# A ramp table written on chip, two small loads on ScalarE's queue, and an earlier place for the first values

## The chip, the cores and the metric

The kernel runs on one core of one Trainium2 chip. The metric is the device time of one execution in microseconds. TensorE is called PE in the rows, VectorE DVE, ScalarE ACT, GpSimd POOL and SyncE SP.

## The reference

One transformer-like block on x of shape (8, 128, 256), all float32:

```
k  = layernorm(x);  v = ctx_2048
y  = wkv(w, u, k, v)          # a scan over the 128 steps, per channel
x1 = x + tanh(g_xattn) * y
f  = fwht(layernorm(x1) * SU_ug) / 64
h  = silu(f @ W_gate.T * (Wscale_gate * 64)) * (f @ W_up.T * (Wscale_up * 64))
out = x1 + tanh(g_ffn) * (fwht(h * SU_dp) / 64 @ W_down.T * (Wscale_dp * 64))
```

In wkv the state decays by exp(w) per step, where w is negative; the numerator collects exp(k)·v and the denominator exp(k), and y is their quotient. For w above zero the kernel adds a correction to k that grows linearly with the step number: minus max(w, 0) times the ramp 0, 1, 2, ... 127.

## The kernel before

The batch of 8 sequences is cut into four groups (0 to 3) of two sequences, 256 tokens each. Every group goes through the same stages: layer norm of x on token rows (`stats1`, `rstd1`, `norm1`), a transposition by PE that puts channels on partitions (`keys`), exp (`keys` on ScalarE), a scan of the denominator (`scan_a`, `mix_den`), the product with the values (`av`), a scan of the numerator (`scan_av`, `mix_num`), a reciprocal by Ln and Exp with one Newton step (`recip`, `error`, `estimate`, `newton`), x1 (`x1`), the Hadamard product (`fwht`), its norm (`square`, `ones`, `rstd2`, `root`, `f_scaled`, `f_hi`, `f_lo`), and then eight slots of gate, up and down products on PE (L900, L938). Each float32 product of the slots is made of three fp32r products of high and low parts.

The weights are prepared on chip in the same head: gate and up weights are transposed and split (`w`, `w_rest`, `w_hi`, `w_lo`), and the down weights go through a Hadamard transformation of butterflies (`fly`, on GpSimd) and PE products (`m`, `m_rest`). So the first 33 us hold the work of group 0 and the preparation, and from there the slots follow one another.

The order on each engine is written out by hand in four tables (`PE_STAGES`, `ACT_STAGES`, `DVE_STAGES`, `POOL_STAGES`); an engine does its list in order and waits on semaphores. On VectorE the head is: stats1 0, setup_rows, norm1 0, setup_shift, stats1 1, center 0, scan_a 0, mix_den 0, av 0, scan_av 0, mix_num 0, norm1 1, estimate 0, newton 0, x1 0, and then the groups after it. On PE it is: keys 0, center, w 0, w_rest 0, w 1, w 2, w 3, w_rest 1 to 3, keys 1, fwht 0, m 0, ones 0, keys 2, m 1. On GpSimd, after eleven memsets: rstd1 0, rstd1 1, fly 0 to 2, error 0, fly 3 to 6.

All loads are issued by SyncE, in this order: the x of group 0 (X, 256 KB), VT (vectors, 17 KB), VR (the row of w, 1 KB), HI (Hadamard and identity matrices, 128 KB), STEP (the ramps, 68 KB, from the host), the x of group 1, the first half of the gate weights (WN, 512 KB), the down weights (DN, 1024 KB), the first half of the up weights (512 KB), the values of group 0 (V, 258 KB), the transposed x of group 0 (XT, 256 KB), the two other halves of the weights, and then the rest of x, V and XT.

The linear correction is a product in `keys` on PE (L809): WPLUS (the negated max(w, 0), its rounded part on partitions 0 and 1, its remainder on partitions 32 and 33) with STEPR, the ramps. `setup_rows` on VectorE makes WPLUS (L612, L615, L619), and the stage `setup` on ScalarE copies STEP to STEPR (L476) after two table loads and two tanh.

Of the kernel before, what the change touches and what calls it, by code (L numbers as in the profile page):

```python
# [5 lines left out]
F32 = mybir.dt.float32  # L6
F32R = mybir.dt.float32r
ALU = mybir.AluOpType
ACT = mybir.ActivationFunctionType

P = 128
NB = 8
C = 256
INTER = 1024
CT = C // P
JT = INTER // P
GB = 2
NG = NB // GB
GT = GB * P
# [116 lines left out]
ON_ACT = {n: places(ACT_STAGES, n) for n in SHARED}  # L136


def build(nc, x, xt, ct, vecs, rows, consts, steps, weights, w_down, out):
    with ExitStack() as stack:  # L140
        def sb(name, shape, dt=F32):
            return stack.enter_context(nc.sbuf_tensor(name, shape, dt))
# [4 lines left out]
        def sem(name):  # L147
            return stack.enter_context(nc.semaphore(name))
# [2 lines left out]
        XT = sb("XT", [P, NG, CT, GT])  # L151
        V = sb("V", [P, NG, CT, GB, PAD])
        VT = sb("VT", [P, NV])
        VR = sb("VR", [CT, P])
        HI = sb("HI", [P, 2 * P])
        HN = sb("HN", [P, P])
        STEP = sb("STEP", [32 + CT, CT, GT])
        STEPR = sb("STEPR", [P, CT, GT], F32R)
        NEGW = sb("NEGW", [CT, P])
        WPLUS = sb("WPLUS", [P, P], F32R)  # L160
        TG = sb("TG", [P, 2])
        DEC, SUMU, CUR, RATIO, MPOS, NEGM, OUTS = (sb(n, [P, CT]) for n in ("DEC", "SUMU", "CUR", "RATIO", "MPOS", "NEGM", "OUTS"))
        NHALF = sb("NHALF", [P, GB])
# [39 lines left out]
        KZ = bank("KZ")  # L203
# [4 lines left out]
        x_in = [sem(f"x{i}_in") for i in range(3)]  # L208
        xt_in = [sem(f"xt{i}_in") for i in range(3)]
        ctx_in = [sem(f"ctx{i}_in") for i in range(3)]  # L210
        const_in, vec_in, row_in, step_in, down_in, stored = (sem(n) for n in ("const_in", "vec_in", "row_in", "step_in", "down_in", "stored"))
        w_in = {(m, h): sem(f"w{m}{h}_in") for m in range(2) for h in range(2)}

        step_clear, plus_clear, pads, d_clear, half, eps_set, ones_set = (sem(n) for n in (
            "step_clear", "plus_clear", "pads", "d_clear", "half", "eps_set", "ones_set"))
        tanh_gate, decay_low, c_ready, m_ready, ratio_ready, decay_set, padded_set, alpha, outs = (sem(n) for n in (
            "tanh_gate", "decay_low", "c_ready", "m_ready", "ratio_ready", "decay_set", "padded_set", "alpha", "outs"))
        neg_ready, signs, wplus, steps_r, centers, at_ready = (sem(n) for n in (
            "neg_ready", "signs", "wplus", "steps_r", "centers", "at_ready"))
# [153 lines left out]
        @block.sync  # L373
        def _(sp):
            def load_x(i):
                b = slice(GB * i, GB * (i + 1) if i < 2 else NB)
                sp.dma_start(X[:, b, :], x[:, b, :]).then_inc(x_in[i], 16)

            def load_xt(i):
                g = slice(i, i + 1 if i < 2 else NG)  # L380
                sp.dma_start(XT[:, g, :, :], xt[:, g, :, :]).then_inc(xt_in[i], 16)

            def load_ctx(i):
                g = slice(i, i + 1 if i < 2 else NG)
                sp.dma_start(V[:, g, :, :, :], ct[:, g, :, :, :]).then_inc(ctx_in[i], 16)

            def load_w(m, h):
                j = slice(h * JT // 2, (h + 1) * JT // 2)
                sp.dma_start(WN[:, m, j, :], weights[:, m, j, :]).then_inc(w_in[m, h], 16)  # L389

            load_x(0)
            sp.dma_start(VT[:, :], vecs).then_inc(vec_in, 16)
            sp.dma_start(VR[:, :], rows).then_inc(row_in, 16)
            sp.dma_start(HI[:, :], consts).then_inc(const_in, 16)
            sp.dma_start(STEP[:, :, :].rearrange("p t n -> p (t n)"), steps).then_inc(step_in, 16)
            load_x(1)
            load_w(0, 0)
            sp.dma_start(DN[:, :, :], w_down).then_inc(down_in, 16)
            load_w(1, 0)
            load_ctx(0)  # L400
            load_xt(0)
            load_w(0, 1)
            load_w(1, 1)
            load_x(2)
            load_ctx(1)
            load_xt(1)
            load_ctx(2)
            load_xt(2)
            for g in range(LAST):
                sp.wait_ge(out_ready, CT * (g + 1))  # L410
                sp.dma_start(out[:, g, :, :], XT[:, g, :, :]).then_inc(stored, 16)
            for t in range(CT):
                sp.wait_ge(out_ready, CT * LAST + t + 1)
                sp.dma_start(out[:, GROUPS[LAST][0]:NG, t, :], XT[:, GROUPS[LAST][0]:NG, t, :]).then_inc(stored, 16)
            sp.wait_ge(stored, 16 * (LAST + CT))

        @block.gpsimd
        def _(pool):
            pool.memset(NHALF[:, :], -0.5).then_inc(half, 1)
            pool.memset(D[:, :, :, :], 0.0).then_inc(d_clear, 1)  # L420
            pool.memset(D0[:, :, :, :], 0.0).then_inc(d_clear, 1)
            pool.memset(STEPR[:, :, :].bitcast(F32), 0.0).then_inc(step_clear, 1)
            pool.memset(WPLUS[:, :].bitcast(F32), 0.0).then_inc(plus_clear, 1)
            pool.memset(SQ[:, 0:1], 0.0).then_inc(pads, 1)
            pool.memset(SP_[:, 0:1], 0.0).then_inc(pads, 1)
            pool.memset(EA[:, :, :, :, 0:1], 0.0).then_inc(pads, 1)
            pool.memset(MEAN[:, :].bitcast(F32), 1.0 / C).then_inc(ones_set, 1)
            pool.memset(ONES[:, :], 1.0 / C).then_inc(ones_set, 1)
            pool.memset(EPSC[:, :], EPS * C).then_inc(eps_set, 1)

            def stage(name, g):
                if name == "rstd1":

                    pool.wait_ge(half, 1)
                    pool.wait_ge(ve1, g + 1)
                    pool.tensor_tensor(RS1[:, GB * g:GB * (g + 1)], VE1[:, GB * g:GB * (g + 1)], NHALF[:, :], ALU.pow).then_inc(rstd1, 1)
                elif name == "fly":
                    fly(pool, g, by_pool["fly"])
                elif name == "norm1":
                    normalise(pool, g, by_pool["norm1"])  # L440
                elif name == "w_lo":
                    split_weight(pool, g, by_pool["w_lo"])
                elif name == "av":
                    multiply_values(pool, g, by_pool["av"])
                elif name == "error":
                    reciprocal_error(pool, g, by_pool["error"])
                elif name == "x_lo":
                    split_x1(pool, g, by_pool["x_lo"])
                elif name == "sum":

                    pool.wait_ge(squared, CT + g)
                    if g > 1:
                        pool.wait_ge(v_full, g)
                    pool.tensor_tensor(FSUM[:, :], FSQ[:, 0, :], FSQ[:, 1, :], ALU.add).then_inc(summed, 1)

            for q in range(-1, SLOTS):
                if q >= 0:

                    n = width(q)
                    pool.wait_ge(h_hi, q + 1)  # L460
                    pool.tensor_tensor(HL[:, q % JT, 0:n], ring(H, q), HH[:, q % JT, 0:n].bitcast(F32), ALU.subtract).then_inc(h_lo, 1)  # L461
                for name, g in POOL_STAGES.get(q, []):
                    stage(name, g)

        @block.scalar
        def _(act):
            def stage(name, g):
                if name == "setup":
                    act.preload_act_table_set("exp_and_others")
# [1 line left out]
                    act.activation(TG[:, 0:1], VT[:, V_GATE:V_GATE + 1], ACT.Tanh, scale=-1.0).then_inc(tanh_gate, 1)  # L471
                    act.activation(TG[:, 1:2], VT[:, V_GATE + 1:V_GATE + 2], ACT.Tanh).then_inc(tanh_gate, 1)
                    act.preload_act_table_set("natural_log_exp_and_others")
                    act.wait_ge(step_clear, 1)
                    act.wait_ge(step_in, 16)
                    act.activation(STEPR[0:32 + CT, :, :], STEP[:, :, :], ACT.Copy).then_inc(steps_r, 1)  # L476

                elif name == "decay":

# [128 lines left out]
        def _(dve):  # L608
            def setup_rows():

                dve.wait_ge(row_in, 16)
                dve.tensor_scalar(NEGW[:, :], VR[:, :], 0.0, -1.0, ALU.max, ALU.mult).then_inc(wplus, 1)  # L612
                dve.wait_ge(wplus, 1)
                dve.wait_ge(plus_clear, 1)
                dve.tensor_copy(WPLUS[0:CT, :], NEGW[:, :]).then_inc(wplus, 1)  # L615
                dve.wait_ge(vec_in, 16)
                dve.tensor_scalar(DEC[:, :], VT[:, V_W:V_W + CT], 0.0, None, ALU.min).then_inc(decay_low, 1)
                dve.wait_ge(wplus, 2)
                dve.tensor_tensor(WPLUS[32:32 + CT, :], NEGW[:, :], WPLUS[0:CT, :].bitcast(F32), ALU.subtract).then_inc(wplus, 1)  # L619

            def setup_shift():

# [168 lines left out]
        def _(pe):  # L791
            def stage(name, g):
                if name == "keys":
# [12 lines left out]
                        pe.wait_ge(wplus, 3)  # L806
                        pe.wait_ge(steps_r, 1)
                    for t in range(CT):
                        i = pe.matmul(KZ[:, t * GT:(t + 1) * GT], WPLUS[:, :], STEPR[:, t, :], start=False, stop=True, skip_group_check=True)  # L809
                    i.then_inc(k_turned, 1)  # L810
                elif name == "center":

# [5 lines left out]
                elif name == "m":  # L818
# [5 lines left out]
                    for i in range(2):  # L824
                        had = HN[:, :] if i and g // 2 else HAD
                        n = 4 * i + 2 * (g % 2)
# [190 lines left out]
```

## Time and profile before

| what | value |
|---|---|
| three timed executions | 117.4, 118.2, 118.34 us; median 118.2 |
| profiled execution, first to last instruction (span) | 117.3 us |
| profiled execution's own time outside the span | the page gives none; the lowest of the three times is 0.1 us above the span, the median 0.9 us |
| busy PE / DVE / ACT / POOL | 99.5 / 70.0 / 67.6 / 61.3 us |
| granted TensorE clock, mean | 0.999 |
| DMA | 7.69 MB, mean 66 GB/s |

The span is what the views of the trace cut into pieces. Busy shares are means over the whole span: in the first quarter PE is about half busy and the DMA engines are full from 5 to 21 us; from 36 us on PE is busy nearly without a break.

### The profile page before, as it was taken

The page shows a single profiled execution, that of the slowest core. Times are in us where ns is not written, and L with a number is a line of the kernel's source. Part 1 is how long each engine was busy: PE and PEld are TensorE (multiplying, and loading weights), DVE is VectorE, ACT ScalarE, POOL GpSimd, SP SyncE. Part 2 cuts the span into 40 slices and gives each one's busy share as a digit, 9 for nine tenths or more (in the row PEclk, how much of TensorE's full clock was granted, in tenths as well). Part 3 has the DMA queues.
Part 4 walks back from the last instruction along what each step waited for, and adds up shares of the span by engine and source line. Part 5 has one row for each costly group of instructions (what it writes and reads, how often), then busy time and mean ns, then how long its engine had stood idle before and what let it go on. Part 6 is the DMA issues. An engine that isn't in the chain of part 4 may idle for free.

```text
span 117.3 us, 1942 instructions
## 1 busy us (share of the span) xinstructions
PE 99.5 (85%) x684; PEld 89.2 (76%) x684; DVE 70.0 (60%) x145; ACT 67.6 (58%) x146; POOL 61.3 (52%) x76
## 2 busy tenths in 40 slices
PE   0056584799969999999999999999999999869980
PEld 0044463664559978789999999999999999769970
DVE  0688289936696798797998456874137531231311
ACT  4589566013689942999562899645459732504400
POOL 7102899689909897953550805732520633222430
PEclk9999999999999999999999999999999999999999
DMA  2799999200000000000000020000020000020002
GB/s 72 171 329 409 334 399 408 101 0 3 0 3 6 0 0 0 0 0 6 0 0 0 3 95 0 0 0 0 6 89 0 3 0 6 0 89 0 3 0 89
DMA packets 3074, 7.69 MB, mean 66 GB/s; under 512 B 468, under 2 KB 854, under 8 KB 2936
## 3 DMA queue, kind: packets, MB, share of 16 engines
q1 hardware_dynamic: 3064, 7.57, 17.9%
q8 instruction: 5, 0.08, 0.3%
q14 instruction: 5, 0.04, 0.1%
HBM read 6.52 MB, written 1.05 MB: 65 GB/s over the span
## 4 chain that ended last, share of the span: by engine, by line
PE 70%; DMA 9%; DVE 8%; ACT 4%; SPq 3%; issue 2%; POOL 1%; POOLq 1%; ACTq 0%; DVEq 0%
PE UG L900 38%; PE OD L938 12%; DMA V<-in_ct 9%; PE KZ L938 6%; PE UG L827 5%; PE FX L859 5%; PE FX L868 2%; DVE X L327 1%; DVE XT L762 1%; PE VB L876 1%; DVE SP_ L640 1%; SPq L389 1%; ACT S L596 1%; DVE OD L705 1%; PE VB L881 1%
## 5 line engine op out<-in xcount | busy, mean ns | idle before, releaser
L461 POOL TENSOR_TENSOR HL<-H,HH 128x256 fp32r<-128x256 f32 x32 | 25.7, 813 | 32.4 <-ACT HH L587 32.4
L776 DVE SCALAR_TENSOR_TENSOR H<-S,ALPHA,UG 128x256 f32<-128x256 f32 x32 | 15.0, 478 | 22.3 <-ACT S L596 22.1
L596 ACT ACTIVATE S<-UG,VT 128x256 f32<-128x256 f32 x32 | 15.1, 472 | 17.5 <-PE UG L900 17.4
L900 PE MATMUL UG<-FH,WTH 128*128 128x256 f32 x128 | 21.4, 289 | 0.8 <-ACT FH L581 0.8
L900 PE MATMUL UG<-FL,WTH 128*128 128x256 f32 x128 | 20.4, 281 | 0.0
L900 PE MATMUL UG<-FH,WTL 128*128 128x256 f32 x128 | 20.3, 280 | 0.0
L900 PEld LDWEIGHTS UG<-FH,WTH 128*128 128x128 f32 x128 | 17.8, 189 | 2.1 <-issue 1.9
L900 PEld LDWEIGHTS UG<-FH,WTL 128*128 128x128 f32 x128 | 17.4, 189 | 0.0
L900 PEld LDWEIGHTS UG<-FL,WTH 128*128 128x128 f32 x128 | 17.4, 188 | 0.0
L587 ACT ACTIVATE HH<-H 128x256 fp32r<-128x256 f32 x32 | 13.2, 412 | 4.5 <-DVE H L776 4.2
L938 PE MATMUL OD<-HH,MH 128*128 128x256 f32 x40 | 11.3, 283 | 1.6 <-DVE XT L762 1.6
L938 PE MATMUL OD<-HH,ML 128*128 128x256 f32 x40 | 11.2, 281 | 0.0
L938 PE MATMUL OD<-HL,MH 128*128 128x256 f32 x40 | 11.2, 280 | 0.0
L803 PE MATMUL KZ<-HI,X 128*128 128x128 f32 x16 | 3.4, 353 | 8.4 <-DVE X L327 8.2
L803 PEld LDWEIGHTS KZ<-HI,X 128*128 128x128 f32 x16 | 2.4, 179 | 9.2 <-issue 8.7
L938 PEld LDWEIGHTS OD<-HH,MH 128*128 128x128 f32 x40 | 7.6, 189 | 1.8 <-DVE XT L762 1.8
L938 PEld LDWEIGHTS OD<-HL,MH 128*128 128x128 f32 x40 | 7.5, 189 | 0.0
L938 PEld LDWEIGHTS OD<-HH,ML 128*128 128x128 f32 x40 | 7.5, 188 | 0.0
L938 PE MATMUL KZ<-HH,MH 128*128 128x256 f32 x24 | 6.9, 289 | 0.4 <-POOL HL L461 0.3
L342 POOL TENSOR_TENSOR DEN<-DEN,R 128x512 f32<-128x512 f32 x4 | 5.2, 1291 | 3.9 <-ACT R L521 3.9
L827 PE MATMUL UG<-DN,HI 128*128 128x512 f32 x12 | 7.1, 712 | 0.0
L938 PE MATMUL KZ<-HH,ML 128*128 128x256 f32 x24 | 6.7, 280 | 0.0
(120 smaller groups left out, 200.5 us busy)
## 6 DMA issues: line engine op xcount, KB each, us to landing
WN<-in_weights SPq DMA_DIRECT2D x4, 512.0 KB, 9.8
DN<-in_w_down SPq DMA_DIRECT2D x1, 1024.0 KB, 8.6
out<-XT SPq DMA_DIRECT2D x3, 256.0 KB, 2.5
V<-in_ct SPq DMA_DIRECT2D x2, 258.0 KB, 10.8
V<-in_ct SPq DMA_DIRECT2D x1, 516.0 KB, 12.5
X<-in_x SPq DMA_DIRECT2D x2, 256.0 KB, 4.2
XT<-in_xt SPq DMA_DIRECT2D x2, 256.0 KB, 10.8
X<-in_x SPq DMA_DIRECT2D x1, 512.0 KB, 11.5
```

Source lines behind the costliest of these rows:

```text
L327: i = eng.tensor_scalar(X[:, n, :], X[:, n, :], MV1[:, n, 0:1], RS1[:, n:n + 1], ALU.subtract, ALU.mult)
L342: eng.tensor_tensor(lanes(DEN[:, g % 2, :, :, :]), lanes(DEN[:, g % 2, :, :, :]), lanes(R0[:, g % 2, :, :, :]), ALU.mult).then_inc(done, 1)
L461: pool.tensor_tensor(HL[:, q % JT, 0:n], ring(H, q), HH[:, q % JT, 0:n].bitcast(F32), ALU.subtract).then_inc(h_lo, 1)
L587: act.activation(HH[:, q % JT, 0:n], ring(H, q), ACT.Copy).then_inc(h_hi, 1)
L596: act.activation(ring(S, q), gate_part(q), ACT.Silu, scale=VT[:, V_SGATE + j:V_SGATE + j + 1]).then_inc(silu_ready, 1)
L776: dve.scalar_tensor_tensor(out=ring(H, q), in0=ring(S, q), scalar=ALPHA[:, j:j + 1], in1=up_part(q), op0=ALU.mult, op1=ALU.mult).then_inc( ...
L803: pe.matmul(KZ[:, t * GT + b * P:t * GT + (b + 1) * P], X[:, GB * g + b, t * P:(t + 1) * P], IDENT, is_transpose=True, start=(t == 0 and b ...
L827: a = pe.matmul(fill(item)[:, :], had, DN[:, n:n + 2, :].rearrange("p j c -> p (j c)"), start=(i == 0), stop=False, skip_group_check=True)
L859: i = pe.matmul(FX[:, o * GT:(o + 1) * GT], AT[:, o, t, :].bitcast(F32), XT[:, g, t, :], start=(o == t == 0), stop=(t == CT - 1), skip_gro ...
L868: i = pe.matmul(FX[:, o * GT:(o + 1) * GT], AT[:, o, t, :], part[:, t, :], start=(n == o == t == 0), stop=(n == 1 and t == CT - 1), skip_g ...
L900: return pe.matmul(dst.rearrange("p (g n) -> p g n", n=GT), w[:, m, j, t, :], f[:, chunks, t, :], start=start, stop=stop, skip_group_check ...
L938: a = pe.matmul(total(g, t), m[:, j, t * P:(t + 1) * P], h[:, j, 0:n], start=(j == 0 and k == 0 and (t == 0 or g == LAST)), stop=(j == JT ...
```

## The change

The ramps are no longer loaded. One ramp of 256 elements (0 to 127, twice) is written to all 128 partitions of STEP by an iota on GpSimd, in place of the memset of STEPR; ScalarE copies it to STEPR, 128x256 in place of 34x512. WPLUS becomes 256 wide with w in one row (partition 0 the rounded part, partition 32 the remainder), and each of the two products of L809 takes its half of WPLUS and the same ramp. VT and VR are issued by ScalarE ahead of its first table load. SyncE issues X group 0, HI, V group 0, the first gate half, X group 1, XT group 0, DN, the first up half, and the rest as before.

```
-            sp.dma_start(VT[:, :], vecs).then_inc(vec_in, 16)
-            sp.dma_start(VR[:, :], rows).then_inc(row_in, 16)
             sp.dma_start(HI[:, :], consts).then_inc(const_in, 16)
-            sp.dma_start(STEP[:, :, :].rearrange("p t n -> p (t n)"), steps).then_inc(step_in, 16)
+            load_ctx(0)
+            load_w(0, 0)
             load_x(1)
-            load_w(0, 0)
+            load_xt(0)
             sp.dma_start(DN[:, :, :], w_down).then_inc(down_in, 16)
             load_w(1, 0)
-            load_ctx(0)
-            load_xt(0)
...
-            pool.memset(STEPR[:, :, :].bitcast(F32), 0.0).then_inc(step_clear, 1)
+            pool.iota(STEP[:, :].rearrange("p (b q) -> p b q", b=GB), [[0, GB], [1, P]], 0, 0, allow_small_or_imprecise_dtypes=True).then_inc(steps_set, 1)
...
         @block.scalar
         def _(act):
+            act.dma_start(VT[:, :], vecs).then_inc(vec_in, 16)
+            act.dma_start(VR[:, :], rows).then_inc(row_in, 16)
...
-                    act.wait_ge(step_clear, 1)
-                    act.wait_ge(step_in, 16)
-                    act.activation(STEPR[0:32 + CT, :, :], STEP[:, :, :], ACT.Copy).then_inc(steps_r, 1)
+                    act.wait_ge(steps_set, 1)
+                    act.activation(STEPR[:, :], STEP[:, :], ACT.Copy).then_inc(steps_r, 1)
...
-                dve.tensor_copy(WPLUS[0:CT, :], NEGW[:, :]).then_inc(wplus, 1)
+                dve.tensor_copy(WPLUS[0:1, :], NEGW[:, :]).then_inc(wplus, 1)
...
-                dve.tensor_tensor(WPLUS[32:32 + CT, :], NEGW[:, :], WPLUS[0:CT, :].bitcast(F32), ALU.subtract).then_inc(wplus, 1)
+                dve.tensor_tensor(WPLUS[32:33, :], NEGW[:, :], WPLUS[0:1, :].bitcast(F32), ALU.subtract).then_inc(wplus, 1)
...
-                        i = pe.matmul(KZ[:, t * GT:(t + 1) * GT], WPLUS[:, :], STEPR[:, t, :], start=False, stop=True, skip_group_check=True)
+                        i = pe.matmul(KZ[:, t * GT:(t + 1) * GT], WPLUS[:, t * P:(t + 1) * P], STEPR[:, :], start=False, stop=True, skip_group_check=True)
```

## Rows read from the trace of the kernel before

**Rows 1.** The page, the chain that ended last, by engine and by line
```profile
PE 70%; DMA 9%; DVE 8%; ACT 4%; SPq 3%; issue 2%; POOL 1%; POOLq 1%; ACTq 0%; DVEq 0%
```
**Rows 2.** The chain in order of time: start us, us, what
```profile
4.76 10.09 DMA V<-in_ct
...
22.16 3.75 PE FX L859 x8
25.91 2.98 PE UG L827 x4
...
44.35 1.73 PE FX L859 x8
```
**Rows 3.** Timeline of VectorE, 11 to 22.2 us: start us, us, instruction [idle before]
```profile
11.76 0.88 DVE L698 SCALAR_TENSOR_TENSOR DEN<-OD,RATIO,SQ 128x256 f32<-128x256 f32 x2
14.87 0.70 DVE L337 TENSOR_TENSOR OD<-OD,V 128x512 f32<-128x512 f32 x1 [2.24 <-DMA V<-in_ct]
...
17.79 2.02 DVE L327 TENSOR_SCALAR X<-X,MV,RS 128x256 f32<-128x256 f32 x2
...
20.53 0.70 DVE L719 SCALAR_TENSOR_TENSOR OD<-DEN,OD 128x512 f32<-128x512 f32 x1
```
**Rows 4.** Timeline of all engines, 0 to 14 us, the same columns
```profile
1.16 0.42 SPq L392 DMA_DIRECT2D VT<-in_vecs  x1
...
1.63 0.32 SPq L393 DMA_DIRECT2D VR<-in_rows  x1
1.68 0.52 POOL L422 MEMSET STEPR<- 128x512 f32 x1
...
2.38 0.28 SPq L395 DMA_DIRECT2D STEP<-in_steps  x1
...
4.09 0.20 ACT L471 ACTIVATE TG<-VT 128x1 f32<-128x1 f32 x1 [2.10 <-DMA VT<-in_vecs]
...
5.07 0.21 DVE L612 TENSOR_SCALAR NEGW<-VR 2x128 f32<-2x128 f32 x1
...
5.32 0.79 POOL L436 TENSOR_TENSOR RS<-VE,NHALF 128x2 f32<-128x2 f32 x1 [2.53 <-DVE VE L674]
...
6.14 0.73 DVE L327 TENSOR_SCALAR X<-X,MV,RS 128x256 f32<-128x256 f32 x2 [0.23 <-POOL RS L436]
6.38 0.63 ACT L476 ACTIVATE STEPR<-STEP 34x512 fp32r<-34x512 f32 x1 [0.69 <-DMA STEP<-in_steps]
...
9.47 0.75 DVE L662 TENSOR_TENSOR AT<-GG,FX 128x256 fp32r<-128x256 f32 x2 [0.28 <-PE FX L816]
```
**Rows 5.** Timeline of PE, 6 to 34 us, the same columns
```profile
7.76 0.77 PE L809 MATMUL KZ<-STEPR,WPLUS 128*128 128x256 f32 x2
8.64 0.80 PE L816 MATMUL FX<-GG,MEAN 128*128 128x256 f32 x2
...
13.55 2.80 PE L841 MATMUL UG<-HI,WN 128*128 128x128 f32 x12 [1.24 <-DMA WN<-in_weights]
...
17.95 0.80 PE L848 MATMUL UG<-WTH,NI 128*128 128x512 f32 x1 [0.75 <-ACT WTH L536]
19.96 1.09 PE L803 MATMUL KZ<-HI,X 128*128 128x128 f32 x4 [1.21 <-DVE X L327]
20.70 0.78 PE L809 MATMUL KZ<-STEPR,WPLUS 128*128 128x256 f32 x2
```
**Rows 6.** Timeline of GpSimd, 11 to 36 us, the same columns
```profile
12.20 3.73 POOL L369 TENSOR_TENSOR DB<-DN 128x512 f32<-128x512 f32 x3 [2.17 <-DMA DN<-in_w_down]
15.88 1.28 POOL L342 TENSOR_TENSOR DEN<-DEN,R 128x512 f32<-128x512 f32 x1
```
**Rows 7.** Windows of the whole core: stretch, length, busy times, clock, DMA share, GB/s
```profile
4.00:5.00 1.00, 0.00 (x0) 0.00 (x0) 0.93 (x5) 0.89 (x3) 0.00 (x0) 1.00 0.62 82
5.00:10.00 5.00, 2.58 (x10) 2.04 (x11) 4.10 (x20) 4.31 (x13) 1.46 (x2) 1.00 0.97 331
```
**Rows 8.** The loads of the tile X, issue to landing
```profile
DMA to landing us min/median/max: 3.2/5.2/11.5
```

More of the change, by code:

```diff
@@ L136, with build @@
 ON_ACT = {n: places(ACT_STAGES, n) for n in SHARED}
-def build(nc, x, xt, ct, vecs, rows, consts, steps, weights, w_down, out):
+def build(nc, x, xt, ct, vecs, rows, consts, weights, w_down, out):
     with ExitStack() as stack:
@@ L153, in build @@
         VT = sb("VT", [P, NV])
-        VR = sb("VR", [CT, P])
+        VR = sb("VR", [1, C])
         HI = sb("HI", [P, 2 * P])
         HN = sb("HN", [P, P])
[L157 to L160, printed above, removed]
+        STEP = sb("STEP", [P, GT])
+        STEPR = sb("STEPR", [P, GT], F32R)
+        NEGW = sb("NEGW", [1, C])
+        WPLUS = sb("WPLUS", [P, C], F32R)
         TG = sb("TG", [P, 2])
@@ L210, in build @@
         ctx_in = [sem(f"ctx{i}_in") for i in range(3)]
-        const_in, vec_in, row_in, step_in, down_in, stored = (sem(n) for n in ("const_in", "vec_in", "row_in", "step_in", "down_in", "stored"))
+        const_in, vec_in, row_in, down_in, stored = (sem(n) for n in ("const_in", "vec_in", "row_in", "down_in", "stored"))
         w_in = {(m, h): sem(f"w{m}{h}_in") for m in range(2) for h in range(2)}
-        step_clear, plus_clear, pads, d_clear, half, eps_set, ones_set = (sem(n) for n in (
-            "step_clear", "plus_clear", "pads", "d_clear", "half", "eps_set", "ones_set"))
+        steps_set, plus_clear, pads, d_clear, half, eps_set, ones_set = (sem(n) for n in (
+            "steps_set", "plus_clear", "pads", "d_clear", "half", "eps_set", "ones_set"))
         tanh_gate, decay_low, c_ready, m_ready, ratio_ready, decay_set, padded_set, alpha, outs = (sem(n) for n in (
@@ L994 @@
     gates = np.concatenate([np.asarray(inputs["g_xattn"]), np.asarray(inputs["g_ffn"])])
-    steps = np.kron(np.eye(CT, dtype=np.float32), np.tile(np.arange(P, dtype=np.float32), GB))
     weights = np.stack([np.asarray(inputs["L0_ffn_W_gate"]), np.asarray(inputs["L0_ffn_W_up"])])
@@ L1002 @@
         "vecs": np.ascontiguousarray(np.concatenate([columns, np.broadcast_to(gates, (P, 2))], axis=1)),
-        "rows": np.ascontiguousarray(np.asarray(inputs["L0_xattn_w"]).reshape(CT, P)),
+        "rows": np.ascontiguousarray(np.asarray(inputs["L0_xattn_w"]).reshape(1, C)),
         "consts": np.ascontiguousarray(np.concatenate([hadamard(P), np.eye(P, dtype=np.float32)], axis=1)),
-        "steps": np.concatenate([steps, np.zeros((32 - CT, CT * GT), np.float32), steps]),
         "weights": np.ascontiguousarray(np.concatenate([
```

## The prediction

> **What bounds the kernel now.** I read the chain that ended last first. By engine it is 70% PE and 9% DMA [rows 1]; the DMA part is one piece in the chain's order of time, the load of V for group 0, 4.76 to 14.85 us [rows 2]. Behind it the chain runs over VectorE to x1, then into fwht 0 on PE at 22.16 us, the m 0 product at 25.91, and from 33 us over the slots, where PE has hardly a gap. So a microsecond won at 22.16 should stay to the end, as no load and no other engine is waited for in a way that doesn't shift with it.
>
> Next the timeline of VectorE. mix_den ends at 12.64, then VectorE stands for 2.24 us until V is there, and av 0 starts at 14.87 [rows 3]. Those 2.24 us are all that an earlier V can give there, since av comes after mix_den in VectorE's list. The rest of the prediction asks what else is late once V is early: the front up to scan_a, the norm1 1 and the Newton step on the way to x1, and PE's own list ahead of fwht 0.
>
> **V and the chain of group 0.** V moves from eighth or ninth place to third. In front of it stand X (256 KB) and HI (128 KB). It would be issued at about 1.6 us and even with the 5.2 us to landing of the middle X load [rows 8] it is there at 6.8 us, 5.8 us ahead of 12.64. So the wait of 2.24 us goes: **−2.24**. What follows takes from av 0 (14.87) to the end of x1 (22.01) 7.14 us, and one piece of it isn't fixed: the two instructions of norm1 1 took 2.02 us here against 0.73 for the same pair at 6.14 [rows 3, 4]. GpSimd was in its butterflies meanwhile. Bounds: 1.29 us better, or as much as one GpSimd instruction (1.28 [rows 6]) worse; I take 0, as GpSimd will be in the butterflies again, and it is the nearest row.
>
> **The front, to scan_a at 10.28.** The small edits:
> - VT and VR leave SyncE's queue and STEP goes: 0.47 + 0.36 + 0.33 = 1.16 us from one issue to the next are gone ahead of the large loads [rows 4]. On ScalarE they put 0.42 + 0.32 = 0.74 us ahead of its first table load; ScalarE idled 2.10 us behind that load, waiting for VT [rows 4], so this is hidden with 1.3 us to spare. VT itself is issued 0.44 us earlier. VT and X now run beside each other: 17 KB against 256 KB is 7% of X's 3.2 us [rows 8], so X group 0 lands between 0 and 0.2 us later; I take 0.1.
> - iota for the memset of STEPR: no row shows an iota. GpSimd starts the memset of 128x512 at 1.68 (0.52 us), ends its memsets at 2.79 and then idles 2.53 us [rows 4]. Nearest rows: a memset of half that size below, a two-operand instruction of 128x512 (1.28 us [rows 6]) above. Either way it is 0, cover 2.5 us. Beyond that each microsecond delays rstd1 0, and so everything. The wider memset of WPLUS adds 0.2 us at most in the same gap.
> - STEPR: ScalarE waited 0.69 us for STEP and copied for 0.63 us [rows 4]. The wait goes and the copy has half the columns (−0.2 to −0.3). So ScalarE's queue (signs, decay, pads) is about 0.9 us, with the earlier VT up to 1.3 us, ahead.
> - setup_rows on VectorE: three instructions on 1x256 in place of 2x128. The first took 0.21 us for 128 columns [rows 4], one of X's norm 0.37 for 256: +0.15 each, +0.45 in all, between 0 and 0.6. VectorE idled 0.23 us before norm1 0 for rstd1 0 [rows 4]; so +0.2 reach norm1 0.
> - The two L809 products keep their size, 0.77 us in keys 0 [rows 5]. Edits of names and the DRAM row of w cost nothing.
>
> What of this reaches scan_a? Before it on VectorE stands center 0, which waited 0.28 us for PE's centre product [rows 4, 5]. PE does keys 0 first. With X and norm1 0 later by 0.1 + 0.2, keys 0 ends at 8.8 instead of 8.53, centre starts at once (the signs are long there, 0.9 us ahead), where before it had waited for them: 8.8 against 8.64, +0.15. So ScalarE's gain of 0.9 us is worth nothing here, since PE and VectorE come last: **+0.1** with rounding.
>
> The third candidate is X group 1, which stats1 1 (7.95) takes ahead of center 0 in VectorE's list. It goes behind V and the first gate half, 770 KB more. At 331 GB/s, the rate from 5 to 10 us [rows 7], this is 2.3 us. Against it: the 1.16 us of issue, and a hole: from 4 to 5 us only 82 GB/s were moved, while STEP and the start of X group 1 were in the queue [rows 7], against 331 behind it, so about 0.7 us are lost. Sum: 7.9 + 2.3 − 1.16 − 0.7 = 8.3 us. The slack is 0.28 us (plus 0.15), up to about 8.3 us. **Cost 0**, bounds −0 and +0.7 (hole not regained).
>
> The Trainium skill, page "DMA: Bandwidth & Descriptors", section "Why a DMA increments its semaphore by 16 and not by 1", says that a load uses the largest number up to 16 of DMA engines that divides its outermost size. For the 34 rows of STEP that is two engines, which fits the hole in the row, and if these two were late in every load behind it, the gain from its removal would be larger than my sum counts. The same page, section "Issuing engines are not separate DMA queues", says that issuing from a second engine saves only the issue time; the 1.16 us of the row are then what the two queues and the dropped load can give.
>
> **The Newton step.** newton 0 (20.53) needs error 0 from GpSimd, which comes after three butterflies, and they wait for DN: 12.20 + 3.73, then 1.28, end 17.16 [rows 6], 5.0 us behind DN. DN goes behind V and XT: 514 KB more, 68 KB less, 446 KB at 331 GB/s: +1.35, less 1.16 and 0.7: it lands at 11.7 in place of 12.2 (11.5 to 13.4 with and without the two credits). error 0 then ends at 16.7, and newton would start at 20.53 − 2.1 = 18.4. It costs nothing until DN lands later than 13.4. XT goes forward too, and nobody waited for it before [rows 3].
>
> **PE's list ahead of fwht 0.** Once x1 is early, this is next. w 1 started at 13.55 after a wait of 1.24 us for the first up half; w_rest 3 ended at 18.75, then 1.21 us of wait for norm1 1, then keys 1 until 21.48, and 0.68 us for x1 [rows 5]. Without the waits keys 1 takes 1.52 us: fwht 0 can't start before the landing of the up half (13.45) + 5.3 + 0.1 + 1.52, that is landing + 6.9. The up half comes right behind DN in both orders, so −0.5 too: 12.95, floor 19.9. x1 ends at 22.01 − 2.24 + 0.1 = 19.9 + a little. So both arrive together. Bounds of the floor: landing 12.8 to 14.6, fwht 0 at 19.7 to 21.5; I take the same value as x1 gives, 20.05 with the usual 0.15 between x1 and PE.
>
> **Sum.** 22.16 − 20.05 = 2.1 us at fwht 0. Behind it m 0 needs butterflies 4 and 6 (they shift with DN, and it has 3.7 us behind fwht's start), keys 2 needs norm1 2, one or two microseconds early before. I cost these at 0; if GpSimd's list shifts by 1.4 instead of 2.1 the slack still covers it. Span 117.3 − 2.1 = 115.2; median 118.2 − 2.1 = **116.1 us**, as the median lies 0.9 above the profiled span.
>
> **Rivals.**
> 1. **TensorE's clock rises sooner.** The eight fwht records took 3.75 us at 22.16 and 1.73 us at 44.35, four m records 2.98 us at 25.91 [rows 2]. The granted column says 1.00 in both, but by the durations the first stretch ran at 1.2 GHz and the later at 2.4 GHz; the change of speed fell into m 0, near 28.5 us, after PE had been busy nearly without a break from 22.16. If with shorter waits between keys 1 and fwht 0 it comes a further 2 us of work sooner than my shift, 1 us more is won: 115.0. The Trainium skill, "TensorE: Matmul & The Clock Gate", section "What's actually happening", says that the clock rises once the array has been kept busy and that the look at it runs freely, not from the kernel's start. By that rule the place differs between executions, in either direction.
> 2. **The clock rises at the same 28.5 us.** Then the 2.1 us of work that would have come after it run at half speed: 1.05 of the gain are given back: 117.1.
> 3. **The loads give it back.** X group 1 lands at 9.0 (+0.7 on scan_a) or the up half at 14.6 (floor 21.5, gain 0.7), or a second GpSimd instruction blocks norm1 1 (+1.3): 117.1 to 117.8. For it: the DMA engines are full from 5 us on, so what is put forward pushes others back. Against: 1.8 us of credits.
> 4. **The change doesn't move V's wait**, another load holds av 0: 118.2. Hardly, since V stands third.
> 5. **The iota is slow**, the case on the slower side. GpSimd does it at 1.68 us ahead of rstd1 0. It decides from 2.5 + 0.5 = 3.0 us on; from there each microsecond goes through norm1 0, keys, scan_a. At 3.0 + 2.1 = 5.1 us the gain is gone; at 7 us the time is 120.1. The rows of GpSimd's instructions of 128x512 (0.52 and 1.28) speak against it; that no iota is in the trace is all that speaks for it.
>
> **Chances.** Forecast (115.3 to 116.9) 0.55; rival 1, 0.17; rival 2, 0.10; rival 3, 0.10; rival 4, 0.03; rival 5, 0.05. About 1% is what a measurement of this kernel tells from no change (117.0 to 119.4). Faster: 0.55 + 0.17 and a little of 3, 0.74; same 0.21; slower 0.05. The range for 8 in 10 takes rival 1 to its end and most of 2 and 3: 115.0 to 117.5.
>
> **What would show it.** In the new profile: the idle time before av 0 is gone and av 0 starts at 12.6 to 12.9; scan_a at 10.3 to 10.5; iota under 1.3 us and rstd1 0 still waiting for VectorE; stats1 1 at about 8.3; the butterflies start at 11.7 to 12.2; w 1 at 13; fwht 0 at 20.05; m 0's change of speed two to three us before 28.5; first slot near 31. The prediction is wrong if av 0 starts early and fwht 0 doesn't follow (PE's list or GpSimd), if scan_a moves by over half a microsecond, or if the stretch from fwht 0 to the end changes in length, which would be the clock.

## The result, and the profile after

The changed kernel takes 117.13 us (median of 20 runs, 115.72 to 117.98) and the kernel before 118.37 us (20 runs, 117.25 to 119.86): ratio 0.985, 95% interval 0.982 to 0.989, or about −1.7 us by the ratio and −1.2 by the medians. The two differ because the ratio leaves out executions more than 1.5% above the fastest of their kernel. The profiled execution took 116.77 us with a span of 115.0, so 1.8 us lie outside the span. The span before was 117.3. The gain is clear of noise, and small: 1.5%, with an interval that ends below 2%.

The page's chain that ended last, after, by engine, and then pieces of it in order of time (start us, us, what), against [rows 1, 2]:

```profile
PE 71%; DVE 15%; ACT 4%; DMA 4%; issue 2%; POOL 1%; POOLq 1%; DVEq 0%; ACTq 0%
```

```profile
0.72 4.10 DMA X<-in_x
...
20.41 3.75 PE FX L858 x8
24.17 2.37 PE UG L826 x4
```

V is out of the chain. The one load that weighs in it is the x of group 0, and VectorE has nearly twice the share. fwht 0 starts 1.75 us sooner than in [rows 2] and takes the same 3.75 us; the m 0 records behind it take 2.37 us instead of 2.98.

The timeline after, 0 to 38 us, for the lines of [rows 3 to 6]:

```profile
0.72 0.41 ACTq L464 DMA_DIRECT2D VT<-in_vecs  x1
...
1.62 0.42 SPq L385 DMA_DIRECT2D V<-in_ct  x1
...
1.78 0.35 POOL L419 IOTA STEP<- 128x256 f32 x1
...
4.85 0.75 DVE L667 BATCH_NORM_STATS2 BS<-X 128x6 f32<-128x256 f32 x2 [4.85 <-DMA X<-in_x]
5.02 0.20 ACT L471 ACTIVATE TG<-VT 128x1 f32<-128x1 f32 x1 [2.02 <-DMA VT<-in_vecs]
...
6.24 0.72 POOL L433 TENSOR_TENSOR RS<-VE,NHALF 128x2 f32<-128x2 f32 x1 [3.43 <-DVE VE L673]
...
6.63 0.42 ACT L475 ACTIVATE STEPR<-STEP 128x256 fp32r<-128x256 f32 x1
6.70 0.41 DVE L618 TENSOR_TENSOR WPLUS<-NEGW,WPLUS 1x256 fp32r<-1x256 f32 x1
...
7.14 0.74 DVE L327 TENSOR_SCALAR X<-X,MV,RS 128x256 f32<-128x256 f32 x2
...
8.75 0.75 DVE L667 BATCH_NORM_STATS2 BS<-X 128x6 f32<-128x256 f32 x2
...
10.67 1.22 DVE L639 TENSOR_TENSOR_SCAN SQ<-D,OD 128x512 f32<-128x512 f32 x1
...
11.66 3.74 POOL L369 TENSOR_TENSOR DB<-DN 128x512 f32<-128x512 f32 x3 [0.83 <-DMA DN<-in_w_down]
...
13.00 2.80 PE L840 MATMUL UG<-HI,WN 128*128 128x128 f32 x12 [0.46 <-DMA WN<-in_weights]
...
13.12 0.70 DVE L337 TENSOR_TENSOR OD<-OD,V 128x512 f32<-128x512 f32 x1
...
16.03 2.03 DVE L327 TENSOR_SCALAR X<-X,MV,RS 128x256 f32<-128x256 f32 x2
...
30.80 0.74 PE L899 MATMUL UG<-FH,WTH 128*128 128x256 f32 x4 [0.78 <-ACT FH L580]
```

The reader is to see two things. av 0 (L337) no longer waits. But stats1 0, the first row of VectorE, starts at 4.85: in the kernel before it starts at 3.93, and norm1 0 follows 2.2 to 2.3 us later in both (6.14 in [rows 4], 7.14 here). The delay is 1.0 us at norm1 0 and at keys 0, 0.80 at stats1 1, 0.70 at PE's centre product, 0.53 at center 0 and 0.39 at scan_a. That, and 0.1 us between mix_den and av 0, is why av 0 gained 1.75 us and not 2.24.

The windows after (columns as in [rows 7]) show the loads as an unbroken stream, 271 GB/s from 4 to 5 us where before there were 82:

```profile
4.00:5.00 1.00, 0.00 (x0) 0.00 (x0) 0.15 (x1) 0.00 (x0) 0.00 (x0) 1.00 0.98 271
5.00:10.00 5.00, 1.97 (x10) 2.00 (x11) 4.62 (x22) 4.87 (x15) 0.72 (x1) 1.00 1.01 369
```

### The profile page after: what moved, and what is told of

The parts are those of the page before. It is cut to its first block, busy times and chain, and to the rows that moved or that the text cites. A ratio compares the mean times of both kernels' runs of the same rounds, so it can differ in the third digit from the quotient of the medians.

```text
span 115.0 us, 1940 instructions
## 1 busy us (share of the span) xinstructions
PE 98.3 (85%) x684; PEld 88.9 (77%) x684; DVE 70.3 (61%) x145; ACT 67.5 (59%) x146; POOL 61.4 (53%) x76
## 3 DMA queue, kind: packets, MB, share of 16 engines
HBM read 6.45 MB, written 1.05 MB: 65 GB/s over the span
## 4 chain that ended last, share of the span: by engine, by line
PE 71%; DVE 15%; ACT 4%; DMA 4%; issue 2%; POOL 1%; POOLq 1%; DVEq 0%; ACTq 0%
PE UG L899 38%; PE OD L937 12%; PE KZ L937 6%; PE UG L826 5%; PE FX L858 5%; DMA X<-in_x 4%; DVE X L327 2%; PE FX L867 2%; DVE BS L667 1%; DVE XT L761 1%; PE VB L875 1%; DVE SP_ L639 1%; DVE SQ L639 1%; ACT S L595 1%; DVE DEN L697 1%
## 5 line engine op out<-in xcount | busy, mean ns | idle before, releaser
L458 POOL TENSOR_TENSOR HL<-H,HH 128x256 fp32r<-128x256 f32 x32 | 25.8, 814 | 32.3 <-ACT HH L586 32.3
L775 DVE SCALAR_TENSOR_TENSOR H<-S,ALPHA,UG 128x256 f32<-128x256 f32 x32 | 15.0, 478 | 22.3 <-ACT S L595 22.2
L937 PE MATMUL KZ<-HL,MH 128*128 128x256 f32 x24 | 6.7, 279 | 0.0
```

Source lines behind the costliest of these rows:

```text
L775: dve.scalar_tensor_tensor(out=ring(H, q), in0=ring(S, q), scalar=ALPHA[:, j:j + 1], in1=up_part(q), op0=ALU.mult, op1=ALU.mult).then_inc( ...
L937: a = pe.matmul(total(g, t), m[:, j, t * P:(t + 1) * P], h[:, j, 0:n], start=(j == 0 and k == 0 and (t == 0 or g == LAST)), stop=(j == JT ...
```

## The experiments

Each was timed beside the kernel before, and the ratios are to it. None leaves out part of the computation. In the tables "slot 0" is the start of the first gate product (before 33.16, after 30.80), "X" the start of the batch norm pair of group 0, both from the profile of one execution. How far such places move by themselves can be seen from kernels with the same loads in the same order: V landed at 14.85 in the kernel before and at 14.73 in the kernel before with three products more on PE (part 4), and DN at 11.04 and 11.74 in the two kernels of part 5. Ratios whose intervals overlap aren't told apart.

**1. Which part carries the gain.** Four kernels on one chip. The first is the kernel before with the new order of the large loads alone:

```
             load_x(0)   # VT, VR, HI, STEP behind it as before
+            load_ctx(0)
+            load_w(0, 0)
             load_x(1)
-            load_w(0, 0)
+            load_xt(0)
             sp.dma_start(DN[:, :, :], w_down).then_inc(down_in, 16)
             load_w(1, 0)
-            load_ctx(0)
-            load_xt(0)
```

> The kernel before with SyncE's large loads in the new order alone (ramps still loaded, VT and VR on SyncE). Theory A, the order carries the gain and X of group 0 lands late only because of VT and VR beside it: X lands at 3.9 again, av 0 starts at 12.6 to 12.9, ratio to before 0.980 to 0.988. Rival B, the dropped load and the shorter queue carry it, as STEP delays all loads behind it by about 1 us: DN and the up half land 1.3 us or more later than before, fwht 0 starts at 21 or later, ratio 0.990 to 1.000.

The second is the changed kernel with these lines back in the old order:

> The changed kernel with the large loads back in the order of before (iota and VT, VR on ScalarE stay). Theory A: V lands about 2 us sooner than before the change through the dropped load (near 13.0), so av 0 starts at 13.0 to 13.3 and half or more of the gain is already here, ratio 0.987 to 0.993. Rival B, the two small edits give everything: ratio below 0.987. Rival C, they give nothing: V at 14.5 or later, ratio 0.997 to 1.008, as X of group 0 lands late.

The third is the changed kernel with VT and VR back on SyncE behind X:

```
             load_x(0)
+            sp.dma_start(VT[:, :], vecs).then_inc(vec_in, 16)
+            sp.dma_start(VR[:, :], rows).then_inc(row_in, 16)
...
-            act.dma_start(VT[:, :], vecs).then_inc(vec_in, 16)
-            act.dma_start(VR[:, :], rows).then_inc(row_in, 16)
```

> The changed kernel with VT and VR back on SyncE right behind X. Theory A, VT beside X on a second queue made X land at 4.8: now 3.9 to 4.1, norm1 0 at 6.3 to 6.5, scan_a at 10.2 to 10.4, fwht 0 0.3 to 0.4 us sooner than in the changed kernel, ratio to before 0.979 to 0.984. Rival B, HI and V close behind X made it late: X at 4.4 or later also here. Rival C, chance between executions: X anywhere, no pattern with the kernels.

The fourth puts the two ScalarE issues behind the first `preload_act_table_set`:

> The changed kernel with VT and VR issued by ScalarE behind its first table load, at about 2.0 us instead of 0.72. Theory A: X lands at 3.9 to 4.1, scan_a at 10.2 to 10.4, ratio 0.979 to 0.984. Rival B, HI and V right behind X: X stays at 4.6 to 4.9 and scan_a at 10.6 to 10.8.

| kernel | ratio, 95% interval | X | av 0 | DN butterflies | fwht 0 | its eight records, us | slot 0 |
|---|---|---|---|---|---|---|---|
| order alone | 0.986 (0.980 to 0.992) | 3.93 | 13.27 | 13.36 | 20.88 | 1.97 | 30.46 |
| old order, rest changed | 0.985 (0.979 to 0.991) | 4.58 | 12.88 | 10.66 | 20.63 | 3.75 | 31.15 |
| VT, VR on SyncE | 0.985 (0.979 to 0.991) | 3.92 | 12.67 | 13.08 | 20.58 | 1.97 | 30.16 |
| VT, VR behind the table load | 0.985 (0.980 to 0.991) | 4.95 | 13.21 | 13.64 | 21.26 | 3.17 | 30.72 |

All four are as fast as the changed kernel, within intervals of about 0.6% to either side. The order alone gives the whole gain, as theory A says, though av 0 starts at 13.27 and not at 12.6 to 12.9. In its one profile fwht 0 starts only 1.28 us sooner than before, and slot 0 is 2.70 us sooner because the fwht records ran at the faster pace; how often they do stays open (part 4). But the old order with the two small edits gives the same, as its rival B had it: V then lands at 12.85 and av 0 starts at 12.88, right behind mix_den. The two parts of the change remove the same wait, so they don't add up.

The edit of the fourth kernel didn't do what it was meant to: ScalarE issues the loads while the table is still being loaded (timeline of that kernel, 0 to 3 us):

```profile
0.72 1.28 ACT L466 ACT_TABLE_LOAD   x1 [0.72 <-PEq L1006]
...
0.75 0.40 ACTq L467 DMA_DIRECT2D VT<-in_vecs  x1
```

So it says nothing of X's delay, and serves as a second look at the changed order: X at 4.95, near the 4.85 of the changed kernel.

In the order-alone kernel the third candidate of the prediction is seen at work (its VectorE timeline): VectorE waits for the x of group 1 and scan_a goes to 10.82.

```profile
9.01 0.75 DVE L668 BATCH_NORM_STATS2 BS<-X 128x6 f32<-128x256 f32 x2 [1.17 <-DMA X<-in_x]
```

With VT and VR back on SyncE, X is at 3.92 and av 0 at 12.67, 0.45 us sooner than in the changed kernel, as theory A has it. But fwht 0, expected 0.3 to 0.4 us sooner, is 0.17 later, since norm1 1 took 2.65 us in place of 2.03 (its VectorE timeline). The ratio of 0.985 misses the expected 0.979 to 0.984.

```profile
15.58 2.65 DVE L327 TENSOR_SCALAR X<-X,MV,RS 128x256 f32<-128x256 f32 x2
```

**2. The small edits alone.** The iota, the single row of w and no ramp load, with all loads on SyncE in the old order:

> The iota, the single row of w and no ramp load alone: all loads on SyncE in the order of before, STEP left out. Theory A, STEP holds up all loads behind it: its removal alone brings V from 14.85 to 13.0 to 13.8 us, av 0 to the same place, fwht 0 to 20.5 to 21.3, ratio 0.984 to 0.993. Rival B, VT and VR off SyncE's queue are as much of it: V at 14.0 or later, fwht 0 at 21.4 or later, ratio 0.992 or more.

Ratio 1.002 (0.998 to 1.006): it gives nothing. Theory A is out, and rival B's figures are met (V at 14.69, fwht 0 at 22.37, ratio above 0.992). Its VectorE timeline and its windows:

```profile
14.71 0.70 DVE L337 TENSOR_TENSOR OD<-OD,V 128x512 f32<-128x512 f32 x1 [2.09 <-DMA V<-in_ct]
```

```profile
4.00:5.00 1.00, 0.00 (x0) 0.00 (x0) 0.95 (x4) 0.78 (x3) 0.00 (x0) 1.00 0.81 114
```

V lands at 14.7 as before, and the hole between 4 and 5 us is still there (114 GB/s, 82 with STEP). So the hole is not STEP's. The removal of its 68 KB and of its issue moved V's landing by 0.16 us, where two executions with the same loads differ by 0.12 (14.85 and 14.73): nothing that one profile can tell.

VT and VR on ScalarE alone, in the kernel before (STEP kept, old order):

```
             load_x(0)
-            sp.dma_start(VT[:, :], vecs).then_inc(vec_in, 16)
-            sp.dma_start(VR[:, :], rows).then_inc(row_in, 16)
...
         def _(act):
+            act.dma_start(VT[:, :], vecs).then_inc(vec_in, 16)
+            act.dma_start(VR[:, :], rows).then_inc(row_in, 16)
```

> The kernel before with VT and VR issued by ScalarE, nothing else (STEP still loaded, order of before). Theory A, shorter SyncE queue and an unbroken stream of loads are worth as much as the order where the order is not changed: V at 12.8 to 13.6 in place of 14.85, X of group 0 at 4.4 to 4.9, ratio to before 0.984 to 0.992. Rival B, it takes the dropped STEP load with it: V at 14 or later, ratio 0.995 to 1.005.

The profile fits theory A: av 0 at 13.33, fwht 0 at 21.09, span 115.8.

```profile
13.33 0.70 DVE L337 TENSOR_TENSOR OD<-OD,V 128x512 f32<-128x512 f32 x1 [0.43 <-DMA V<-in_ct]
```

The times don't: ratio 0.999 (0.994 to 1.004), with medians of 118.17 against 119.01. The one profiled execution was at 117.56 us among the faster ones. How much of its gain is regular stays open. So neither small edit alone has a gain that the times show, and both together have the whole: with both, V is issued 1.24 us sooner than before (3.52 against 4.76) and lands 2.00 us sooner. What is sure is that the order of the loads needs neither.

**3. Why X of group 0 lands late.** HI, and with it every load behind it on SyncE, held back until GpSimd's second clearing memset is done, with VT and VR beside X:

```
+            sp.wait_ge(d_clear, 2)
             sp.dma_start(HI[:, :], consts).then_inc(const_in, 16)
```

> The changed kernel with one wait of SyncE on GpSimd's second clearing memset (it ends near 1.75 us) between X of group 0 and HI; VT and VR stay on ScalarE beside X. Theory A, HI and V issued close behind X keep X's last packets: X lands at 3.9 to 4.2, norm1 0 at 6.2 to 6.6. Rival B, a second queue beside SyncE's makes it late: X stays at 4.5 to 4.9.

And VT and VR held back in the same way, with HI and V close behind X:

```
+            act.wait_ge(d_clear, 2)
             act.dma_start(VT[:, :], vecs).then_inc(vec_in, 16)
```

> The changed kernel with ScalarE waiting for GpSimd's second clearing memset (1.75 us) before it issues VT and VR; SyncE is untouched, HI and V close behind X. Theory A, a second queue beside X's packets makes X late: X at 3.9 to 4.3. Rival B, HI and V issued close behind X do it alone: X at 4.6 to 4.9. Both count if it is between.

X at 4.42 in the first and at 4.61 in the second (VT issued at 1.77 there), where both together, with V third, give 4.78 to 4.95 and neither 3.90 to 4.04 in seven kernels (before, the same with the products of part 4, order alone, VT and VR on SyncE, the iota alone, and the two of part 5). The first lies between the ranges of its two theories. The second is at the edge of rival B's, HI and V alone, but it isn't a clean test, as VT was still in flight beside X from 1.77 on. Taken together they say that both count. Of HI and V, HI isn't the one: with VT and VR on ScalarE in the old order (part 2), HI stands 0.44 us behind X too, and X is at 4.42 as in the first. The times were 0.996 (0.990 to 1.001) and 0.989 (0.983 to 0.995). The first is slower than the changed kernel for another reason, which its VectorE timeline shows: the x of group 1 came at 10.36.

```profile
10.38 0.75 DVE L668 BATCH_NORM_STATS2 BS<-X 128x6 f32<-128x256 f32 x2 [1.98 <-DMA X<-in_x]
...
14.63 0.70 DVE L337 TENSOR_TENSOR OD<-OD,V 128x512 f32<-128x512 f32 x1
```

V was there at 5.87, and still av 0 started where it started before the change, since stats1 1 stands ahead of scan_a in VectorE's list. This is rival 3 of the prediction, carried out. In the second the late VT had a price: tanh started at 6.08, scan_a at 11.38 and av 0 at 13.83.

**4. TensorE's clock.** Three float32 products whose results nobody reads, put into PE's idle times of the changed kernel, in the stage list behind w_rest 0, ahead of w_rest 3 and behind keys 1:

```
+                elif name == "fill":
+                    pe.wait_ge(const_in, 16)
+                    pe.wait_ge(ones_set, 2)
+                    for n in g:      # (128,), (256,), (192,)
+                        pe.matmul(VB[:, 0:n], ONES[:, :], HI[:, 0:n], start=True, stop=True)
```

> The changed kernel with three float32 products on PE whose results nobody reads (128 columns behind w_rest 0, 256 ahead of w_rest 3, 192 behind keys 1). Theory A, the place where TensorE reaches its upper clock is a term of its own of 1 to 3 us: the rise comes ahead of or within the first records of fwht 0, these take 1.7 to 2.2 us in place of 3.75, first slot at 29.0 to 29.6 in place of 30.80 (GpSimd's last butterfly, 27.3, and the products behind it are then the floor), ratio to before 0.967 to 0.977. Rival B, the place of the rise doesn't hang on what PE did before fwht 0: records of 427 ns pitch up to 25 us, and the time is that of the changed kernel or up to 0.5 us worse.

In its profile (PE's timeline) even the weight transpositions ran at the pace of 2.4 GHz, and fwht 0 too:

```profile
13.20 1.50 PE L845 MATMUL UG<-HI,WN 128*128 128x128 f32 x12 [0.80 <-DMA WN<-in_weights]
...
20.61 1.96 PE L863 MATMUL FX<-XT,AT 128*128 128x256 f32 x8 [1.02 <-DVE XT L726]
...
26.41 0.63 PE L802 MATMUL KZ<-HI,X 128*128 128x128 f32 x4 [1.26 <-POOL X L327]
...
29.63 0.63 PE L904 MATMUL UG<-FH,WTH 128*128 128x256 f32 x4
```

slot 0 is at 29.63, 1.2 us sooner than after, and the six times lie within 0.5 us (115.61 to 116.11), where the twenty of the changed kernel spread over 2.3. The six of the first kernel of part 5, without such products, lie within 0.75 us on the same chip, so the narrow spread isn't shown to be theirs. The ratio is 0.983 (0.978 to 0.988), short of the expected 0.967 to 0.977; the interval overlaps that of the changed kernel. The third row says why no more comes of it: PE now waits 1.26 us for norm1 2, which GpSimd does.

The same products in the kernel before:

> The kernel before with the same three unread products on PE. It shows what of the change is left when TensorE's rise no longer differs. Theory A: the rise comes before fwht 0 (22.2), the records of fwht 0 take 1.7 to 2.2 us, first slot at 30.6 to 31.5 in place of 33.16, ratio to before 0.978 to 0.988, and the changed kernel with the same products is 1.0 to 1.8 us faster than this. Rival B, the longer wait ahead of fwht 0 lets the clock fall again or keeps it low: first slot after 32.5, ratio 0.995 or more.

Ratio 0.989 (0.981 to 0.997), 117.54 us, between the two theories. The profiled execution, at 118.41 us the slowest of the six, shows what rival B feared, with slot 0 at 32.38: the records of keys 1 at 19.7 have the fast pace, the last unread product is slow again (0.84 us against 0.49 in the changed kernel), and so is fwht 0 behind it.

```profile
19.66 0.63 PE L803 MATMUL KZ<-HI,X 128*128 128x128 f32 x4 [1.49 <-DVE X L327]
...
21.86 3.75 PE L864 MATMUL FX<-XT,AT 128*128 128x256 f32 x8 [0.56 <-DVE XT L727]
```

The windows of this execution (first) and of the kernel before (second), with the granted clock third from the end, tell two slow stretches apart:

```profile
22.20:25.90 3.70, 3.70 (x9) 2.83 (x9) 1.80 (x10) 0.25 (x1) 2.46 (x3) 0.50 0.02 8
22.20:25.90 3.70, 3.70 (x9) 2.98 (x10) 2.10 (x11) 0.00 (x0) 2.16 (x3) 1.00 0.01 3
```

The fwht records take 3.75 us in both. Where the clock has not risen yet, the column reads 1.00; where it had risen and fell, it reads 0.50, here from 20.2 to 27.0 us. Three more profiles have such a fall over fwht 0, all without unread products: the old order with both small edits (from 19.0 to 25.8), the iota alone (20.9 to 27.7), and VT and VR on ScalarE alone (19.1 to 25.9). All four have the old order of the loads. Three others without unread products had fwht 0 at the fast pace (order alone, VT and VR on SyncE, HI held back). So filled idle times don't fix the clock, and whether they move the odds isn't shown.

The mean granted clock of an execution shows the fall too: 0.967 to 0.971 in the four profiles that have it, 0.996 or more in the ten others. Of the twenty executions of the changed kernel six read 0.968 or 0.969; they took 117.6 to 118.0 us, and the median of the other fourteen is 116.6. In the kernel before, beside the experiments, 23 of 51 read so, and on each of three chips their median is 1.0 to 1.2 us above that of the others. It was six of six in the old order with both small edits, none of six with the order alone, and none of twelve in part 5. So the order of the loads may pay through the clock as well; no run here separates this.

With the products on both sides the change is worth 0.989 against 0.983, on two chips and with intervals that overlap, so the 1.0 to 1.8 us of theory A aren't shown.

**5. An order with DN ahead of V.** All on SyncE. V only needs to be there by mix_den's end, so the down weights go ahead of it:

```
             load_x(0)        # then VT, VR, HI
             load_x(1)
             load_w(0, 0)
             sp.dma_start(DN[:, :, :], w_down).then_inc(down_in, 16)
             load_ctx(0)
             load_w(1, 0)
             load_xt(0)
```

> VT and VR on SyncE, iota, and the order X, VT, VR, HI, X of group 1, first gate half, DN, V, first up half, XT. Theory A: V needs only to be there by 12.6, and the loads of the weights are worth more in front: X at 3.9, DN at 11.2 to 11.7, V at 12.0 to 12.7, up half at 13.2 to 13.6, fwht 0 at 19.8 to 20.2, ratio 0.975 to 0.983 (with the clock's rise as in the changed kernel). Rival B, V lands after 13: av 0 late and fwht 0 at 20.4 or later.

Ratio 0.980 (0.975 to 0.985), 115.65 us, as theory A had it. X at 4.04, V there at 11.72, av 0 at 12.31, butterflies from 11.11, fwht 0 at 19.96, slot 0 at 29.56. PE's timeline shows no idle time ahead of fwht 0, so it is PE's list that comes last there, 6.27 us behind w 1:

```profile
19.96 3.49 PE L857 MATMUL FX<-XT,AT 128*128 128x256 f32 x8
```

With the three unread products as well:

> The version with V behind DN, VT and VR on SyncE, with the three unread products on PE. Theory A: TensorE reaches the upper clock before fwht 0, this takes under 2.2 us, and the first slot starts at 28.6 to 29.5; ratio to before 0.970 to 0.979. Rival B, GpSimd's butterflies and norms are the floor already at 29.5: ratio 0.979 to 0.985, no better than without them.

Ratio 0.974 (0.968 to 0.980), 115.21 us, the lowest of all and as theory A had it, on another chip than the 0.980, whose interval it overlaps. It is clear of the changed kernel's 0.982 to 0.989; the 0.980 isn't quite. slot 0 is at 28.93.

```profile
20.53 1.89 PE L862 MATMUL FX<-XT,AT 128*128 128x256 f32 x8
...
28.93 0.63 PE L903 MATMUL UG<-FH,WTH 128*128 128x256 f32 x4
```

**The floor below.** In the five kernels where fwht 0 was fast or nearly so and GpSimd didn't idle, slot 0 follows the first butterfly by the same time: 13.36 → 30.46 (order alone), 13.08 → 30.16 (VT, VR on SyncE), 13.64 → 30.72 (behind the table load), 15.04 → 32.15 (HI later), 11.81 → 28.93 (the last): 17.08 to 17.12 us. That is GpSimd's list from DN's landing on: four butterflies and error 0, three butterflies, two rstd1, norm1 2, butterfly 7, and behind it PE's m 1 and m_rest 0. In the changed kernel it would give 11.66 + 17.1 = 28.8 against the 30.80 reached at the lower clock. The changed kernel with the unread products didn't come to it: 11.85 → 29.63 is 17.78 us, as GpSimd idled 0.17 and 0.44 us there until VectorE, behind x1, had the variances. So with TensorE at 2.4 GHz early, a load put ahead of DN costs its full time only where GpSimd doesn't wait for x1 in any case.

## Why the prediction was right

The forecast was −2.1 us, 116.1 within 115.0 to 117.5; measured −1.7 by the ratio and 117.13. The median lies inside the range, but outside the band of 115.3 to 116.9 that had the largest chance, and on the number of rival 2 (117.1), whose mechanism the profile doesn't show: the clock didn't rise at 28.5. The mechanism was the forecast's: V's wait went, and fwht 0 followed. Two terms were mis-sized, and one credit was right in its sum for a wrong reason. That the profiled span came out as forecast (115.0 against 115.2) is in part luck: fwht 0 gained 1.75 us and not 2.1, and the clock added 0.6 that stood at 0.

- **V's wait, −2.24:** gone in full. V landed at 5.97.
- **The front, +0.1:** it was +0.39 at scan_a (+0.48 at av 0 against 12.64). The term mis-sized is "X group 0 lands between 0 and 0.2 us later; I take 0.1": it was 0.92. I scaled by bytes (17 KB against 256). Experiments 1 to 3 show that it takes VT and VR beside X, for 0.5 us, and V close behind it for the rest. On the way from norm1 0 to scan_a the delay fell from 1.0 to 0.39: PE's centre product had waited 0.39 us for ScalarE before and doesn't now, and the rest went at its end and at center 0, which had waited 0.28.
- **setup_rows, +0.45 and 0.2 at norm1 0:** the last of the three instructions ended at 7.11, norm1 0 started at 7.14 with rstd1 0 ready at 6.96; so +0.18 there, as forecast. The three instructions together took 0.26 us more, not 0.45.
- **iota:** 0.35 us in GpSimd's gap. Right, rival 5 is out.
- **ScalarE 0.9 us ahead:** wrong. VT landed 0.9 us later than in [rows 4], not earlier (tanh at 5.02 against 4.09), so STEPR was made at 6.63 against 6.38. It cost nothing, as PE and VectorE came last, as forecast.
- **X group 1, 8.3 us:** landed at 7.87; stats1 1 started at 8.75, since VectorE was late itself. Cost 0 in this order, but 1.2 and 2.0 us of waiting in two of the experiments and 0.5 in two more: it stands closer to the edge than I had it.
- **The Newton step and DN at 11.7:** 11.66. The up half at 12.95: w 1 at 13.00. The sum held, its credit didn't: I gave 0.7 us for the hole to STEP, and experiment 2 shows the hole without STEP. In the changed kernel the hole is filled all the same. From 4 to 5 us the kernels with V ahead of the first gate half moved 190 to 288 GB/s and those with the x of group 1 issued at 1.63 or 2.01 us 262 and 228; those with it issued at 2.39 or later in V's place moved 82 to 188. Why isn't shown. By the Trainium skill, "DMA: Bandwidth & Descriptors", section "Why a DMA increments its semaphore by 16 and not by 1", STEP's 34 rows go through two DMA engines; if this delays what is behind, then the one pair of profiles shows no more of it than the 0.16 us by which V landed sooner without STEP.
- **norm1 1 at 2.02 again:** 2.03 here, but 1.7 to 2.7 in the experiments. **PE's floor of 19.9:** keys 1 was done by 19.7, and x1 came last, at 20.27. The floor itself was put half a microsecond too high: where PE's list came last, fwht 0 began 6.27 us behind w 1 (part 5), against 6.8 in the sum, which would be 19.3 here.
- **fwht 0 at 20.05:** 20.41.
- **Behind fwht 0, 0:** the stretch to slot 0 shrank from 11.0 to 10.4 us, because the clock rose at about 25.4 instead of 28.3, that is 5.0 us into fwht 0 and m 0 instead of 6.1. This is rival 1 in part, and by the prediction's own sign (the stretch from fwht 0 to the end changes in length) its zero for the clock was wrong, by 0.6 us. In the experiments the clock rose for good at 10.8, at 18.2 to 20.2, within fwht 0, or within m 0, and in four it had risen and fallen again before fwht 0 (part 4). Of the three kernels with products in PE's idle times two had the fast pace at fwht 0 and one hadn't, so it can't be set in this way. The Trainium skill's rule ("TensorE: Matmul & The Clock Gate", section "What's actually happening"), that the look at PE's activity runs freely, agrees with this spread; no run here can show it by itself.
- **The sum against the median:** I put the median 0.9 us above the profiled span. With the 1.8 us outside the span that the changed kernel's execution shows, the profiled execution before was probably one of about 119.1 us, above its median. This isn't measured, as the first profile's own time isn't known, but every execution of the experiments for which both numbers are there has 1.7 to 1.9 us outside its span. It would be most of why 2.3 us of span are 1.2 to 1.7 us of time.

Not forecast was the equivalence: nothing in the prediction said that the two small edits and the order remove the same wait.

## What to carry to other kernels

Where a change has several parts that all bring one late transfer forward, they pay for one wait together; ask of each what it gives when the others are there. Put a load just ahead of the time at which its user is free, not at the front: V third landed 7 us before av 0 could start (5.97 against 13.02). In the order of part 5, fwht 0 came 0.6 us sooner than with V third and the same small edits (19.96 against 20.58); in the times (0.980 against 0.985) this isn't clear of noise. In this kernel the first load of the chain was hurt by what was issued close behind it or beside it by far more than its share of the bytes. And look at the granted clock of every execution: here it parts the times of one kernel by about 1 us, as much as most of these changes are worth.

## What the runs showed of the hardware

- 17 KB beside 256 KB on a second queue, and larger loads issued 0.44 us behind it, delayed the 256 KB by 0.9 us together (3.90 to 4.82), and by 0.5 us with the 17 KB alone beside it. With the larger loads behind it and the 17 KB 1.05 us later it was 0.7.
- A DMA issue that stands behind a table load in ScalarE's program went out 0.03 us after the table load's start, and not after its 1.28 us.
- An iota of 128x256 float32 took 0.35 us on GpSimd, where the memset of the same size behind it took 0.31.
- Eight fwht records took 3.75 us at the lower clock and 1.9 to 2.0 us at the higher. Ahead of the first rise the granted clock reads 1.00 although the pace is the lower one; after a fall it reads 0.50.
- The two norm1 1 instructions on VectorE (128x256 float32) took 1.7 to 2.7 us while GpSimd was in its butterflies, and 0.73 us where GpSimd was idle (norm1 0).
